# Causal attention on one core: the order of diagonal and off-diagonal score units in the second half of the queries

## What is computed

```
scores = einsum('bhqd,bhkd->bhqk', Q, K)
scores = clip(scores, -80.0, 80.0)
scores = where(causal, scores, -inf)
weights = softmax(scores / sqrt(d_qk), axis=-1)
attn = einsum('bhqk,bhkd->bhqd', weights, V)
return attn @ W_O
```

## Time and profile before

| | us |
|---|---|
| median of 3 runs | 436.92 |
| lowest and highest | 436.18, 437.71 |
| the profiled execution | 439.81 |
| its span, first to last instruction | 438.1 |
| attention, first scores to last weighing | 10.96 to 341.56 |

### The profile page before, as it was taken

The page is one execution under the profiler, slowest core; times in us unless marked ns, Lnnn a source line. Parts: engine busy times, 40 slices in busy tenths (PEclk is TensorE's granted clock), DMA queues, the critical chain, the costliest instruction groups (busy, mean ns, idle before and its releaser), DMA issues. The chain is left out here.

```text
span 438.1 us, 12095 instructions
## 1 busy us (share of the span) xinstructions
PE 406.7 (93%) x4139; PEld 222.8 (51%) x4139; DVE 373.8 (85%) x816; ACT 351.6 (80%) x560; POOL 173.1 (40%) x164
## 2 busy tenths in 40 slices
PE   8899999999999999899999999999998798699993
PEld 5533344444434354344344444343343697699993
DVE  3979799999999999979999999999998687367674
ACT  3879999999889989798899999989986464366662
POOL 8221001331553022507601322454001576678887
PEclk9889999999999999899999999999999999799998
DMA  5268501676066155401940760067214456567640
GB/s 154 54 170 196 155 1 49 145 176 194 2 160 181 49 114 125 104 1 30 211 101 1 170 151 21 2 145 197 72 41 121 116 156 173 145 175 214 189 139 19
DMA packets 33004, 50.60 MB, mean 116 GB/s; under 512 B 5627, under 2 KB 16545, under 8 KB 32944
## 3 DMA queue, kind: packets, MB, share of 16 engines
q1 hardware_dynamic: 25488, 36.51, 33.7%
q10 hardware_dynamic: 5184, 9.05, 7.2%
q0 software_dynamic: 2272, 4.27, 3.0%
HBM read 21.35 MB, written 5.33 MB: 61 GB/s over the span
## 5 line engine op out<-in xcount | busy, mean ns | idle before, releaser
L1048 ACT ACTIVATE prob<-ring 128x1024 f32<-128x1024 f32 x288 | 273.1, 1047 | 26.3 <-PE ring L1237 25.2
L1255 PE MATMUL o_acc<-prob,v_stat 128*32 128x512 f32 (+3 forms) x1536 | 156.0, 502 | 6.5 <-ACT o_sb L1079 5.1
L1237 PE MATMUL ring<-queries,keys 32*128 32x512 f32 (+3 forms) x1536 | 129.0, 384 | 3.6 <-DVE whole_q L658 3.0
L1237 PEld LDWEIGHTS ring<-queries,keys 32*128 32x128 f32 x1536 | 72.3, 186 | 88.7 <-issue 48.1
L698 DVE TENSOR_SCALAR prob<-prob 128x2048 f32<-128x2048 f32 x64 | 77.4, 1219 | 4.9 <-ACT prob L1048 4.6
L712 DVE SCALAR_TENSOR_TENSOR prob<-prob,mask_hi 128x1024 f32<-128x1024 f32 (+1 forms) x80 | 81.0, 1013 | 0.0
L1133 ACT ACTIVATE prob<-ring,b1T 128x128 f32<-128x128 f32 x156 | 44.5, 368 | 39.2 <-issue 17.8
L711 DVE TENSOR_SCALAR prob<-prob 128x1024 f32<-128x1024 f32 (+1 forms) x80 | 64.9, 811 | 4.0 <-ACT prob L1048 4.0
L1255 PEld LDWEIGHTS o_acc<-prob,v_stat 128*32 128x32 f32 x1536 | 34.4, 109 | 61.6 <-issue 42.4
L591 POOL DMA_INDIRECT by_expert<-xrow,index x32 | 43.5, 1360 | 46.0 <-DVE index L809 38.4
L572 POOL TENSOR_TENSOR rstd<-var_eps,const 128x4 f32<-128x4 f32 x8 | 17.1, 2134 | 92.4 <-DVE var_eps L757 92.4
(11 more groups left out here) (114 smaller groups left out, 330.2 us busy)
## 6 DMA issues: line engine op xcount, KB each, us to landing
queries<-query_parts SPq DMA_DIRECT2D x60, 256.0 KB, 4.0
v_stat<-in_w ACTq DMA_DIRECT2D x34, 256.0 KB
keys<-key_parts SPq DMA_DIRECT2D x60, 128.0 KB, 2.4
queries<-by_expert SPq DMA_DIRECT2D x39, 66.0 KB
xrow<-in_x_rows SPq DMA_DIRECT2D x8, 264.0 KB, 4.7
xT<-in_x_T SPq DMA_DIRECT2D x8, 256.0 KB, 3.1
v_stat<-in_w SPq DMA_DIRECT2D x5, 256.0 KB
out<-prob,queries POOLq DMA_INDIRECT x39
```

The costliest lines, as they stand in the source:

```text
L1048: act.activation(prob[u % P_SLOTS][:, 2 * half:2 * half + 2, :].rearrange("p h s -> p (h s)"), slot(("score", u, half))[:], ACT.Exp, scale ...
L1237: last = pe.matmul(out[:, j % 2 * QC + off:j % 2 * QC + off + w], keys[hg][r, kt * P:(kt + 1) * P], queries[hg][r, qc, part, QC - w:QC], s ...
L1255: last = pe.matmul(o_acc[j * VW:(j + 1) * VW, QC - w:QC], v_stat[b % 2][:, hg, kt, j, :], prob[u % P_SLOTS][:, j, off:off + w], start=begi ...
```

## The change

`unit_table` lists the units of a half in another order. Off-diagonal units of both groups are put in one list `off`, the five diagonal units in another, `on`; the half starts with one off-diagonal unit, then each diagonal unit is preceded by one more off-diagonal unit, and the rest of `off` follows. With A and B for off-diagonal units of the first and second group, D for a full diagonal unit, M for the one with 128 and 384 columns and S for the shared one, the second half went A A A A D M S B B B B D M and now goes A A D A M A S B D B M B B. The first half has no off-diagonal units, and its order D M S D M stays. All else is the same code.

```
     for qc in range(NQC):
         d = qc * QC // P
-        own = [[(qc, [(i, kt, 0, QC)]) for kt in range(d + 1)] +
-               [(qc, [(i, d + 3, 0, P), (i, d + 1, P, 3 * P)])] for i in range(2)]
-        out += own[0] + [(qc, [(0, d + 2, 0, 2 * P), (1, d + 2, 2 * P, 2 * P)])] + own[1]
+        off = [(qc, [(i, kt, 0, QC)]) for i in range(2) for kt in range(d)]
+        on = [[(qc, [(i, d, 0, QC)]), (qc, [(i, d + 3, 0, P), (i, d + 1, P, 3 * P)])] for i in range(2)]
+        on = on[0] + [(qc, [(0, d + 2, 0, 2 * P), (1, d + 2, 2 * P, 2 * P)])] + on[1]
+        out += off[0:1]
+        for n in range(len(on)):
+            out += off[1 + n:2 + n] + on[n:n + 1]
+        out += off[1 + len(on):]
     return out
```

## The result

| | before | after |
|---|---|---|
| median, us | 437.31 of 4 runs (436.18 to 439.01) | 445.16 of 4 runs (443.00 to 448.46) |
| ratio, 95% interval | | 1.0191 (1.0143 to 1.0238) |
| the profiled execution, its span | 439.81, 438.1 | 448.46, 446.7 |
| attention, first scores to last weighing | 10.96 to 341.56 | 11.8 to 345.55 |
| from there to the end | 96.5 | 101.2 |

The change costs 7.85 us where 2.7 was forecast and 441.8 was the end of the range. Two more chips ran the changed kernel beside the one before: 1.0134 (1.0090 to 1.0178), +6.5 us, and 1.0102 (1.0066 to 1.0139), +4.4 us. The direction was right each time, every size was above the forecast, and the first chip's was the largest. So there are two questions: what the order costs wherever it runs, and what came on top.

The account below looks back on a forecast made before the run. No single engine bounds it: exponentials pace units without side jobs, PE those with jobs, DVE three waits. Terms 0 + 0.6 + 1.9 + 0.2 = 2.7 us, added to median 436.92, give 439.6; 8-in-10 range 436.7 to 441.8.

Parts of the forecast that it names:

- First term: Batches 1 to 3, n = 7 to 12: rotation 0.61 later, absorbed by PE's idle 1.00 at n = 15; sum 0.
- Second term: Batches 1 to 3, n = 15 to 19: M clip holds its weighing about 0.3; 0.2 taken each, 0.6 in all.
- Third term: Batches 0 to 2, n = 31 to 35: rotation 0.34 later, rank matmul 0.63 later; 1.9 in all, bounds 1.0 to 3.1.
- a bound of 0.4: At n = 31: POOL's power or cast takes 0.4 out of the D clip, making each boundary 1.04.
- Nothing at 28 to 30: Count of clip work up to each n, second pair: DVE is no later than before at n = 28 to 30.
- the prediction listed three: Batch 1 places where PE waits behind DVE's clips: rotation at n = 11, scores of n = 15, rank matmul at n = 35.
- Fourth term: End of batch 3: rotation 0.34 later, a little given back by lighter scores; +0.2, bounds -0.4 and +0.6.
- (a): Rival, chance 0.22: no measurable change; ACT's pause at n = 19 goes (437.6) or the n = 10 cast ends early (438.1).
- the signs of being wrong: Rank matmul not held, ACT's pause at n = 19 gone, or weighings of n = 18 to 22 earlier than their distance allows.
- (b): Rival, chance 0.08: faster, 434.5, because the diagonal run at n = 18 to 23 really holds PE.
- (c): Rival, chance 0.12: POOL lands between the halves of the D clips at 13 and 31 each time; up to 6.0, 442.9.
- The remark: Cast after n = 10 ends about 2 us sooner, saving DVE's 0.5 pause; the sum would be 1.2.

Follow-up runs that it names:

- e13: The kernel before with the D unit of n = 27 moved to n = 25 in the second pair of batches 0 to 2: 431.13 us, 1.0020.
- the order by load: The kernel before, reordered by counting DVE's clip work ahead of each wait: 431.49 us, 0.9878 on one chip; 426.73 us, 0.9917 on another.
- e10: The kernel before with the D unit of n = 34 moved to n = 31 in the second pair, M left last: 438.23 us, 1.0066.
- e11: The kernel before with the changed order only in the second pair of batches 0 to 2: 439.84 us, 1.0085.
- e9: First run of the order by load, the kernel before reordered by DVE's clip work ahead of each wait: 431.49 us, 0.9878.
- e12: The order by load plus 20 unread matmuls on PE ahead of the last batch's rotation at n = 33: 430.33 us, 0.9862 of the kernel before.
- e14: The kernel before, unchanged, run for its profile on the third chip: 430.94 us, 1.0006.
- e15: The changed kernel, unaltered, on the third chip beside the kernel before: 435.35 us, 1.0102.
- e1: The changed kernel, unaltered, run again on the second chip beside the kernel before: 436.89 us, 1.0134.
- e8: The kernel before with all off-diagonal units first and diagonal units last in the second half of both pairs: 430.57 us, 0.9980.
- e16: The order by load again, unchanged, on another chip against the kernel before: 426.73 us, 0.9917.

## Why the prediction was wrong

**First term (n = 7 to 12), 0: right.** The rotation moved by 0.61, and PE's idle time at n = 15 shrank by 0.75.

**Second term (n = 15 to 19), 0.6: direction right, size off.** The M clip held its weighing by 0.42, not 0.3, since POOL also lengthened the D clip of n = 13 (130.44, 1.10). That was inside the bounds. The choice of 0.2 leaned on ACT's pause hiding part of the hold. On three other chips there is no such pause to hide in, and the interval shows 0.4: 1.2 in all.

**Third term (n = 31 to 35), 1.9: the step that failed.** Both waits are there, in the order and with the distances foretold. Each boundary costs 1.14 and not 0.63, beyond the upper bound of 1.04. The rank's share was right (0.28 against 0.29). The rotation's was 0.75 against 0.34, for two reasons. 0.10 is the power of the variance, in the D clip now; I had it as a bound of 0.4 and gave the case 0.12. In its old place it already cost 0.3, of which the earlier trace rows shows 0.14 (normalizing of 1.54 where the earlier trace rows has 1.40). 0.30 is the cast on the division, which the count could not contain, since it adds up lengths of clips and takes all else for fixed. "Nothing at 28 to 30" was the false sentence. The last 0.1 comes from the same cast: it holds the scores of n = 28 behind the rotated queries, a fourth place where PE waits for DVE, and the prediction listed three. So the cast costs 0.4 of the 1.14, as much as e13 shows for it alone.

**Fourth term, +0.2: right,** 24.3 against 24.1, for profiles without the low clock. With it 1.4 to 1.5 more can stand in either kernel, and I had no term for that at all. The profile before showed another low stretch, at the start of batch 2, which cost 2.7 and which I took for a disturbance. It was one, of a kind that the first chip has in both kernels. It stands behind a pause of ACT with its operand ready, in the kernel before

```profile
180.46 0.60 ACT L1079 ACTIVATE o_sb<-o_acc 128x512 f32<-128x512 f32 x1 [1.16 <-remote]
...
184.00:186.00 2.00, 2.00 (x16) 0.51 (x8) 1.62 (x4) 1.26 (x2) 0.00 (x0) 0.50 0.03 8
```

and in the changed one (ACT, then a window, columns as above), where it cost 2.5:

```profile
98.66 1.94 ACT L1053 ACTIVATE prob<-ring 128x1024 f32<-128x1024 f32 x2 [0.96 <-PE ring L1242]
...
104.00:106.00 2.00, 2.00 (x16) 0.51 (x8) 2.00 (x3) 1.28 (x2) 0.00 (x0) 0.50 1.05 316
```

**The sum.** With the measured terms it is 0 + 1.2 + 3.4 + 0.2 = 4.8, and the third chip's 4.4 agrees. Added to the 436.92 of the prediction that would be 441.7, just inside the range. So the third term accounts for most of the gap between 2.7 and 4.8, and what put the first chip's time outside is what came on top, for which the prediction had no term: the low clock of the last half and the start of the expert layer. The second chip's +6.5 is near that and the low clock of its last half, 6.3, if its timed runs were like the profiled one. The first chip's +7.85: its two profiles differ by 8.6 in span. Of that 4.0 lie in attention up to the last weighing: 3.4 for the boundaries, less 1.1 around n = 11 to 25, where ACT's pauses near n = 19 are in the profile before and not in that after, and 1.7 for the last half, low clock included; the low stretches at the start of a batch (2.5 against 2.7) and the rest cancel. The other 4.6 lie in the expert layer, which waits for ACT's copy. It took 92.4 to 95.6 in the twelve profiles of the three chips without pauses of ACT, 94.2 to 97.8 in four of a chip that has them, and 96.5 and 101.2 in these two. One kernel alone, the order by load, had 97.3 and 92.4. So this part goes with chip and execution. In all eighteen profiles its length goes with the time that PE stands at the lower level in it, the last 8 us left out: 92.4 without such a stretch, 93.6 to 94.2 with one of 3.4 us, 95.6 with two, 96.5 and 96.7 with one of 6.8, 97.3 and 97.8 with both kinds, and 101.2 with two of 6.8, one of which begins at 351.9, in the second of the two waits of PE behind the late copy. But these are single profiles, and what holds ACT there was not found. That the first chip's timed runs differ by 7.85 for the same reasons is likely and not shown; both profiled executions stand above their medians, by 2.5 and 3.3.

**The rivals.** (a) was right in one thing, and with it one of the signs of being wrong came: the pauses at n = 19 were gone in the profile after, and the three stretches around it came out 1.1 shorter in all for it, not longer. But e10 and e11, with the old order at n = 5 to 17, and e9 and e12, with another one, have such pauses on one chip, and no order has them on three others: they don't belong to the diagonal run. (b): no weighing of n = 18 to 23 was the bound. (c) was the nearest: POOL did land between the halves of both D clips every time, and its price was 0.1 and about 0.1 and not 0.4. The remark that by the rule of the Trainium skill (SBUF — State Buffer, Who interferes with whom), that the order of issue decides, the cast after n = 10 would end 2 us sooner did not come out. It took 3.88 for 4.48, but only because it started 0.60 later: counted from n = 5 it ends at 20.55 in both kernels (e14, e15). It was again passed over at the first boundary, and DVE still stood idle 0.51 for it,

```profile
126.01 0.69 DVE L693 TENSOR_TENSOR query_parts<-whole_q,query_parts 128x512 fp32r<-128x512 f32 x1 [0.51 <-POOL query_parts L588]
```

so it gained nothing.

## What to carry to other kernels

When an order of equal work is changed, list the places where the pacing engine waits for another one, also those where it has a few tenths to spare, and count the work queued ahead of each; put the light items there, and check the items just behind too. The order by load did this and gained 1%, while taking turns lost 1 to 2%. Such a count gives the sign and not the size where instructions of a second engine lengthen those of the first: a shift of 0.34 moved one of them onto its neighbour's and cost as much again. And an interval between two like points of the trace, with undisturbed clock, resolves 0.05 us where medians of ten runs resolve about 1.

## What the runs showed of the hardware

POOL and DVE delay each other by the place of the boundary between two DVE instructions. An instruction of DVE that has started keeps its time (0.42 with a cast of POOL starting 0.29 later). One that starts 0.04 after the cast takes 0.85. A cast of POOL took 0.61 on a transpose or a short operation, and 3.88 and 4.48 across clips, while the power, 2.48 or 2.75, ended 0.04 behind the end of the first DVE instruction in its way, one half of a D clip or a whole clip. Why the one is passed over and the other is not, no run shows.

PE fell to its lower level, 1.2 GHz, for 3.4 us at a time after idle times of 1.30 and 1.48 in six of sixteen profiles, and did not after 1.30 to 1.48 in the other ten. The same wait can cost 1.4 to 1.5 more or nothing.

ACT stood still for 0.45 to 0.70 at n = 19, with scores ready, in the profile before and in all four of the chip of e9 to e12, and in none of the twelve of three other chips (e1 to e8, e13 to e16). On the same two chips it also stood still for 0.96 to 1.16 at the start of a batch in three profiles (before, after, e11), each time with a low stretch of PE 2 to 4 us behind it that cost 2.5 to 2.7, and for 2.43 at the last copy in the profile after. Its cause is open; nothing was tried against it.
